# The first cross attention of a Perceiver kernel, its steps of one key group put together into rounds of two

## What is computed

```python
def _L0_xattn_ref(x, y, wq, bq, wk, bk, wv, bv, wo, bo):
    N_HEADS, D_EMBED, D_HEAD = 16, 256, 16
    B, SQ, _ = x.shape
    SKV = y.shape[1]
    q = (x @ wq + bq).reshape(B, SQ, N_HEADS, D_HEAD)
    k = (y @ wk + bk).reshape(B, SKV, N_HEADS, D_HEAD)
    v = (y @ wv + bv).reshape(B, SKV, N_HEADS, D_HEAD)
    scores = jnp.einsum('bqhd,bkhd->bhqk', q, k) / jnp.sqrt(jnp.asarray(D_HEAD, x.dtype))
    attn = jax.nn.softmax(scores, axis=-1)
    out = jnp.einsum('bhqk,bkhd->bqhd', attn, v).reshape(B, SQ, D_EMBED)
    return out @ wo + bo

x = x + _L0_xattn_ref(_layernorm(x, axis=-1), ctx_768, ...)
```

## Time and profile before

| | |
|---|---|
| runs | 2088.68, 2086.16, 2082.78 us |
| profiled execution, own time | 2083.18 us |
| its span, first to last instruction | 2081.4 us |
| TensorE busy | 1893.3 us, 91% |
| VectorE, ScalarE, GpSimd busy | 1301.7, 924.8, 678.0 us |
| first look_at to last look_at of this stage | 31.36 to 692.65 us |
| project of the last tile | 717.86 us |
| granted TensorE clock, mean | 0.955 |

### The profile page before, as it was taken

One profiled execution on the slowest core, in us unless ns is written; L12 is line 12 of the kernel. 1 busy time (PEld: TensorE's weight loads), 2 busy tenths in 40 slices (PEclk: granted clock), 3 DMA queues, 4 the chain that ended last, 5 costly groups with the idle time before them and its releaser, 6 DMA issues.

```text
span 2081.4 us, 44041 instructions
## 1 busy us (share of the span) xinstructions
PE 1893.3 (91%) x17906; PEld 1569.1 (75%) x17906; DVE 1301.7 (63%) x2827; ACT 924.8 (44%) x1952; POOL 678.0 (33%) x762
## 2 busy tenths in 40 slices
PE   6999999999999688795999999999999989779994
PEld 4777777777777477685999999999999846546662
DVE  5777877777777765543767667676676536532222
ACT  4666666666665423343444444444444324212221
POOL 4444444444443322104323333233333014130002
PEclk9999999999999888887999999999999989799997
DMA  6211111111200200104223222232222070310002
GB/s 199 65 34 34 34 57 42 34 34 34 65 2 3 93 1 1 49 1 113 56 56 90 77 56 56 56 97 70 56 56 56 1 280 2 121 59 31 31 29 71
DMA packets 55655, 119.81 MB, mean 58 GB/s; under 512 B 4432, under 2 KB 41888, under 8 KB 53920
## 3 DMA queue, kind: packets, MB, share of 16 engines
q1 hardware_dynamic: 53920, 112.80, 18.1%
q0 software_dynamic: 1536, 4.20, 0.6%
HBM read 107.80 MB, written 9.18 MB: 56 GB/s over the span
## 4 chain that ended last, share of the span: by engine, by line
PE 72%; DVE 15%; ACT 6%; issue 4%; DMA 1%; POOL 1%; SPq 0%; POOLq 0%; DVEq 0%; ACTq 0%
PE ps L104 8%; PE ps L163 7%; PE ps L433 6%; PE ps L2106 6%; PE ps L472 5%; DVE arena L531 4%; PE ps L1314 4%; PE ps L456 4%; PE ps L2130 3%; PE ps L1315 3%; PE ps L450 2%; DVE arena L1407 2%; PE ps L1272 2%; PE ps L1300 2%; PE ps L1299 2%
## 5 line engine op out<-in xcount | busy, mean ns | idle before, releaser
L531 DVE TENSOR_REDUCE arena<-ps 128x1 f32<-128x400 f32 (+1 forms) x512 | 258.4, 567 | 136.8 <-PE ps L433 136.8
L651 ACT ACTIVATE arena<-ps 128x384 f32<-128x384 f32 (+1 forms) x512 | 223.4, 522 | 102.5 <-PE ps L456 102.5
L1314 PE MATMUL ps<-arenaR 128*128 128x386 f32 x768 | 246.5, 356 | 1.1 <-DVE arenaR L1401 1.1
L1500 ACT CAST arenaR<-ps 128x512 fp32r<-128x512 f32 (+1 forms) x256 | 116.7, 508 | 225.0 <-PE ps L163 225.0
L1315 PE MATMUL ps<-arenaR 128*128 128x256 f32 x768 | 215.6, 281 | 0.0
L557 DVE TENSOR_TENSOR arena<-arena 128x512 f32<-128x512 f32 x192 | 176.7, 920 | 5.3 <-ACT arena L651 1.7
L1543 POOL TENSOR_TENSOR arenaR<-h,arenaR 128x400 fp32r<-128x400 f32 (+1 forms) x60 | 57.9, 964 | 370.5 <-ACT arenaR L1485 370.5
L709 POOL TENSOR_TENSOR arena<-arena 128x512 f32<-128x512 f32 (+1 forms) x96 | 134.0, 1396 | 101.9 <-ACT arena L651 99.5
L1401 DVE TENSOR_TENSOR arenaR<-ps,arenaR 128x512 fp32r<-128x512 f32 (+1 forms) x256 | 138.8, 584 | 25.3 <-ACT arenaR L1500 24.9
L682 POOL TENSOR_TENSOR arenaR<-arena,arenaR 128x400 fp32r<-128x400 f32 x64 | 67.1, 1049 | 256.1 <-ACT arenaR L617 255.8
L1383 DVE TENSOR_TENSOR arenaR<-wsb,arenaR 64x400 fp32r<-64x400 f32 x64 | 66.0, 1035 | 133.3 <-ACT arenaR L1486 133.3
(11 more groups left out here) (316 smaller groups left out, 4591.6 us busy)
## 6 DMA issues: line engine op xcount, KB each, us to landing
wsb<-in_ctx SPq DMA_DIRECT2D x16, 1152.0 KB
arena<-in_ctxT SPq DMA_DIRECT2D x16, 800.5 KB, 5.0
arena<-in_ctxT SPq DMA_DIRECT2D x32, 400.2 KB, 7.2
wsb<-in_ctxT SPq DMA_DIRECT2D x32, 400.2 KB, 7.5
gu<-in_m_gu SPq DMA_DIRECT2D x8, 1536.0 KB, 19.6
h<-in_ctxT SPq DMA_DIRECT2D x15, 800.5 KB, 5.0
dn<-in_m_dn SPq DMA_DIRECT2D x8, 768.0 KB, 9.2
xs_rows<-zeros SPq DMA_DIRECT2D x1, 2944.0 KB, 15.7
```

The lines of the kernel that those rows point to most:

```text
L531: e.tensor_reduce(mx4[n % 2][:, u, i:i + 1], ps[:, at("look", n, i, u), 0:400 + (i == 3)], AX.X, ALU.max).then_inc(c.maxed.at((n, i, u)), 1)
L651: e.activation(v[:, u, 0:128 * GN[s]], ps[:, at("st", n, s, u), 0:128 * GN[s]], ACT.Exp).then_inc(c.exp_a.at((x0, n, s, u)), 1)
L1314: e.matmul(o, PTh[:, t, :], v[:, t, 0:386], start=(t == 0), stop=False)
```

## The change

The loops of all engines run over rounds r of two key groups in place of steps of one. In round r TensorE does: scores of the first group, look_at of one chunk, values of both groups of round r - 1 (and total behind those of a second half), scores of the second group, look_at of another chunk; then the turn, two chunks of keys, two pieces of vals, and now and then queries or project.

With it: the sums of values leave bank 7. Each round's sums take a bank of the ring, which is now round all 8, and ScalarE copies it out (`take_sum`) to new tiles `va` (first half of the unit) and `vb` (second half, with the denominators). `normalise` reads those, adds the halves with one more instruction and divides. The gathering of sums of P is shared otherwise: VectorE has 4 adds a unit where it had 7, GpSimd 6 where it had 4. The projection is added to x on VectorE one round after TensorE made it, and TensorE's `project` stands at the end of a round r divisible by 8, in which `normalise` of the unit it needs also stands.

```diff
     V = [ar(128, KT, 256) for _ in range(2)]
     P = [ar(128, 4, 512) for _ in range(3)]
     acc_d, acc_p = ar(128, 4, 128), ar(128, 4, 128)
+    va, vb = ar(128, 128), ar(128, 256)
...
     N = 2 * NB
     G0, GN = (0, 4, 7, 10), (4, 3, 3, 3)
-    FIRST, LAST = -6, 16 * (NT - 1) + 18
+    FIRST, LAST = -3, 2 * N
...
+    def groups(r):
+        return [(r // 2, 2 * (r % 2) + i) for i in range(2)] if 0 <= r < 2 * N else []
+    def looks(r):
+        return [((r + 3) // 2, 2 * ((r + 3) % 2) + i) for i in range(2)] if 0 <= (r + 3) // 2 < N else []
+    def keys_of(r):
+        return [((r + 4) // 2, 2 * (r % 2) + i) for i in range(2)] if 1 <= (r + 4) // 2 < N else []
+    def vals_of(r):
+        b, p = (r + 4) // 4, 2 * ((r + 4) % 4)
+        return [(b, i) for i in (p, p + 1) if i < 7] if 0 <= b < NB else []
+    def turns(r):
+        return (r + 1) // 2 if r % 2 and 0 <= (r + 1) // 2 < N else None
+    def asks(r):
+        return (r + 5) // 8 if (r + 5) % 8 == 0 and 1 <= (r + 5) // 8 < NT else None
+    def projects(r):
+        return r // 8 - 1 if r % 8 == 0 and 1 <= r // 8 <= NT else None
     bank = {}
     def at(*use):
         if use not in bank:
-            bank[use] = len(bank) % 7
+            bank[use] = len(bank) % 8
         return bank[use]
     for i in range(4):
         at("k", 0, i)
-    at("v", 0, 0)
+    for i in range(2):
+        at("v", 0, i)
...
+    for r in range(FIRST, LAST + 1):
+        for i in range(2):
+            for n, s in groups(r)[i:i + 1]:
+                for u in range(4):
+                    at("st", n, s, u)
+            for n, k in looks(r)[i:i + 1]:
+                for u in range(4):
+                    at("look", n, k, u)
+            if i == 0 and r >= 1:
+                at("sum", r - 1)
+        if turns(r) is not None:
+            at("m", turns(r))
+        for use in keys_of(r):
+            at("k", *use)
+        for use in vals_of(r):
+            at("v", *use)
+        if asks(r) is not None:
+            at("q", asks(r))
+        if projects(r) is not None:
+            at("o", projects(r))
...
-    def splits(s):
-        b, i = (s + 14) // 8, (s + 14) % 8
-        return (b, i // 2) if i % 2 == 0 and 1 <= b < NB else None
+    def splits(r):
+        b, i = (r + 7) // 4, (r + 7) % 4
+        return (b, i) if 1 <= b < NB else None
...
-        def values(n, s):
+        def values(r):
+            n, half = r // 2, r % 2
             b, f = n // 2, 128 * (n % 2)
-            w.wait_ge(*c.exp_a((x0, n, s, 3)))
+            w.wait_ge(*c.exp_a((x0, n, 2 * half + 1, 3)))
             w.wait_ge(*v_out((b, 6)))
-            if s == 0 and n:
-                w.wait_ge(*c.o_out((x0, n - 1)))
-            for t in range(GN[s]):
-                k = G0[s] + t
-                r = 128 if k < 12 else KL
-                for u in range(4):
-                    a = e.matmul(ps[32 * u:32 * u + 32, 7, 0:128], V[b % 2][0:r, k, f + 32 * u:f + 32 * u + 32],
-                                 P[(4 * n + s) % 3][0:r, u, 128 * t:128 * t + 128], start=(k == 0), stop=(k == 12))
-            a.then_inc(c.summed.at((x0, n, s)), 1)
-        def total(n):
-            w.wait_ge(*added_d((n, 3)))
-            w.wait_ge(*added_p((n, 3)))
-            w.wait_ge(*padded("rows"))
-            for a, v in enumerate((acc_d, acc_p)):
-                for u in range(4):
-                    o = e.matmul(ps[32 * u:32 * u + 32, 7, 128:256], ones, v[:, u, :], start=(a == 0), stop=(a == 1))
-            o.then_inc(totals.at(n), 1)
+            bk = take("sum", r)
+            for s in (2 * half, 2 * half + 1):
+                for t in range(GN[s]):
+                    k = G0[s] + t
+                    rows = 128 if k < 12 else KL
+                    for u in range(4):
+                        a = e.matmul(ps[32 * u:32 * u + 32, bk, 0:128], V[b % 2][0:rows, k, f + 32 * u:f + 32 * u + 32],
+                                     P[(4 * n + s) % 3][0:rows, u, 128 * t:128 * t + 128], start=(k == 7 * half), stop=(k == 6 + 6 * half))
+                a.then_inc(c.summed.at((x0, n, s)), 1)
+            if half:
+                w.wait_ge(*added_d((n, 3)))
+                w.wait_ge(*added_p((n, 3)))
+                w.wait_ge(*padded("rows"))
+                for a, v in enumerate((acc_d, acc_p)):
+                    for u in range(4):
+                        o = e.matmul(ps[32 * u:32 * u + 32, bk, 128:256], ones, v[:, u, :], start=(a == 0), stop=(a == 1))
+                o.then_inc(totals.at(n), 1)
+            emptied[bk] = c.o_out((x0, r))
...
+        for r in range(FIRST, LAST + 1):
+            for i in range(2):
+                for use in groups(r)[i:i + 1]:
+                    scores(*use)
+                for use in looks(r)[i:i + 1]:
+                    look_at(*use)
+                if i == 0 and r >= 1:
+                    values(r - 1)
+            if turns(r) is not None:
+                turn_m(turns(r))
+            for use in keys_of(r):
+                keys(*use)
+            for use in vals_of(r):
+                vals(*use)
+            if asks(r) is not None:
+                queries(asks(r))
+            if projects(r) is not None:
+                project(projects(r))
...
-                for t in range(2):
+                for t in range(2 if s == 2 else 1):
                     w.wait_ge(*added_d.now())
                     e.tensor_tensor(acc_d, acc_d, v[:, :, 128 * t:128 * t + 128], ALU.add).then_inc(added_d.at((n, s)), 1)
         def normalise(n):
             b, g = n // 2, n % 2
             q = slice(64 * (b % 2), 64 * (b % 2) + 64)
-            w.wait_ge(*totals(n))
-            e.reciprocal(rS, ps[:, 7, 128:256]).then_inc(c.dv.at(), 1)
+            w.wait_ge(*c.o_out((x0, 2 * n + 1)))
+            e.reciprocal(rS, vb[:, 128:256]).then_inc(c.dv.at(), 1)
+            e.tensor_tensor(oS, va, vb[:, 0:128], ALU.add).then_inc(c.dv.at(), 1)
             w.wait_ge(*c.dv.now())
-            e.tensor_tensor(oS, ps[:, 7, 0:128], rS, ALU.mult).then_inc(c.o_out.at((x0, n)), 1)
-            w.wait_ge(*c.o_out((x0, n)))
+            e.tensor_tensor(oS, oS, rS, ALU.mult).then_inc(c.dv.at(), 1)
+            w.wait_ge(*c.dv.now())
             w.wait_ge(*c.in_const("small"))
             e.tensor_scalar(o1, oS[:, 0:64], c.par[:, 0:1], c.bvc[:, g:g + 1], ALU.mult, ALU.add).then_inc(c.dv.at(), 1)
             w.wait_ge(*c.dv.now())
...
+        for r in range(FIRST, LAST + 1):
+            if asks(r - 1) is not None:
+                queries(asks(r - 1))
+            if projects(r - 1) is not None:
+                project(projects(r - 1))
+            for use in looks(r)[:1]:
+                maxima(*use)
+            for use in groups(r)[:1]:
+                add(*use)
+            for use in looks(r)[1:]:
+                maxima(*use)
+                if use[1] == 3:
+                    maximum(use[0])
+            if r >= 2 and r % 2 == 0:
+                normalise(r // 2 - 1)
+            for use in groups(r)[1:]:
+                add(*use)
+        project(projects(LAST))
...
+        def take_sum(r):
+            n = r // 2
+            w.wait_ge(*(totals(n) if r % 2 else c.summed((x0, n, 1))))
+            if n:
+                w.wait_ge(*c.o_norm((x0, n - 1)))
+            v = vb if r % 2 else va
+            e.copy(v, ps[:, at("sum", r), 0:256 if r % 2 else 128]).then_inc(c.o_out.at((x0, r)), 1)
...
+        for r in range(FIRST, LAST + 1):
+            for use in groups(r)[:1]:
+                exps(*use)
+            if r >= 1:
+                take_sum(r - 1)
+            for use in groups(r)[1:]:
+                exps(*use)
+            if turns(r) is not None:
+                turn_m(turns(r))
+            for use in keys_of(r):
+                keys(*use)
+            if splits(r) is not None:
+                split(*splits(r))
+            for use in vals_of(r):
+                vals(*use)
...
-                r = 128 if s < 3 else KL
-                w.wait_ge(*added_p.now())
-                e.tensor_tensor(acc_p[0:r], acc_p[0:r], v[0:r, :, 256:384], ALU.add).then_inc(added_p.at((n, s)), 1)
+                for t in range(2 if s == 2 else 1, GN[s]):
+                    k = 128 if G0[s] + t < 12 else KL
+                    w.wait_ge(*added_p.now())
+                    e.tensor_tensor(acc_p[0:k], acc_p[0:k], v[0:k, :, 128 * t:128 * t + 128], ALU.add).then_inc(added_p.at((n, s)), 1)
...
+        for r in range(FIRST, LAST + 1):
+            for use in groups(r)[:1]:
+                add(*use)
+            if r % 2 == 0 and 1 <= (r + 4) // 2 < N:
+                blockdiag((r + 4) // 2)
+            for use in groups(r)[1:]:
+                add(*use)
+            if splits(r) is not None:
+                split(*splits(r))
...
```

More of the change, by code:

```diff
@@ L305, in latents @@
     at("q", 0)
-    for s in range(FIRST, LAST + 1):
-        if has_look(s):
-            for u in range(4):
-                at("look", *look(s), u)
-        if has_key(s):
-            at("k", *key(s))
```

(76 more changed lines are left out.)

20 lines of the change are left out of this document (removed).

## The result

The changed kernel took 2078.22 us (median of 8 runs, 2073.04 to 2081.89) against 2086.78 beside it: ratio 0.9963, interval 0.9949 to 0.9977. Faster, but by 8.6 us where 41 were forecast.

A forecast was written before the change was run, and what follows sets the result against it. TensorE's own work was taken as the bound, some 40.8 of 42.6 us a batch. 42.6 - 2.8 - 1.8 + 2.1 = 40.1 over 15 batches, with the ends 40 us less in all: 2045 us, range 2033 to 2057.

The forecast's parts named there:

- (b): End of a round with project: TensorE waits for VectorE's normalise, 1.0 us once in two batches, 0.5 a batch.
- the walk: Even round followed in us from its first scores: TensorE reaches project at 10.1, VectorE's normalise ends at 11.1.
- (c): Odd round's first maxima queue behind normalise and an add on VectorE, whose adds stretch beside GpSimd: 1.0 us a batch.
- Changes of cut: TensorE switching between whole array, rows and columns: four a round, not eight; 0.70 us less, 2.8 a batch.
- The waits of before: TensorE's waits for VectorE in the kernel before (maxima, values and total), all taken off: 1.8 us a batch.
- (a): Values wait for the sums' bank, still read by exponentials of the round's first scores: 0 to 0.15 us, 0.4 a batch.
- (d): Short round: the next look waits for the bank that ScalarE's copy of vals, behind split, frees late: 0.2 us a batch.
- The ends: Start and end of the stage: fewer changes at the start save 1 us, fewer VectorE adds at the end 1.5.
- rival B: VectorE and GpSimd block each other in the even round: waits 4.0, 42.0 us a batch, 2075 us; chance 0.14.
- A: TensorE alone sets the rate: waits 0.5, 38.5 us a batch, 2021 us; chance 0.27.
- C: Late maxima hold banks: TensorE waits 2.7 us twice a batch, 5.5 with (a); 43.5 a batch, 2097 us; chance 0.06.
- D: Looks behind scores still show weight loads (sign: a look at 0.89): 41.6 us a batch, 2068 us; chance 0.08.

The follow-up runs named there:

- e1: The changed kernel with TensorE's project one round later: 2052.78 us, ratio 0.9857 to the kernel before.
- e10: The changed kernel with normalise ahead of the second look's maxima on VectorE in even rounds, project left in place: 2057.85 us, ratio 0.9869.
- e2: The changed kernel with the adds of P shared as before, 7 a unit on VectorE and 4 on GpSimd: 2075.38 us, ratio 0.9954.
- e3: The changed kernel with GpSimd's adds after the first of a unit cut to one column in 128: 2063.69 us, ratio 0.9914.
- the extra matmul: Two runs on e1 with one more 64-column matmul a round between the chunks of keys: on one strip 2074.02 us, on the whole array 2061.47 us.
- e11: The changed kernel with both moves, normalise ahead of the second maxima and project one round later: 2052.36 us, ratio 0.9839.
- e4: The changed kernel with look_at ahead of scores in both halves of a round, the ring's order swapped likewise: 2117.30 us, ratio 1.0148.
- e12: e10 with the bank of a round's sums dealt ahead of the scores' banks: 2237.77 us, ratio 1.073.
- e9: e1 with normalise moved to the end of odd rounds, va and vb doubled, project two rounds later: 2087.68 us, ratio 1.0011.

## Why the prediction was wrong

The forecast was 2.5 us a batch over 15 batches. Measured over the same 15, from first scores to first scores: 42.5 - 41.8 = 0.7. The failed step is (b), the price of project's wait. I gave it 1.0 a pair; the changed kernel without it (e1) is 4.0 a pair and 25.4 us faster, and e10, which removes the wait otherwise, 20. Over the 15 batches that is 25.6 us where I had 7.5: 18 of the 27 us by which they fell short. Two things were missing in (b):

- Its first part was 2.2 and not 1.0. Counted from a round's first scores, the walk had the second maxima end at 7.9, the maximum at 8.5, normalise at 11.1, and TensorE ready at 10.1. In the round before the wait that ends at 310 they are 8.1, 9.8, 12.6 and 10.4. So nearly all of it is the maximum, 1.7 for 0.6, by one subtraction. I had seen that two-input instructions are stretched and put 0.3 on each in (c), a mean that takes in times with GpSimd idle. But the place is fixed: GpSimd's two adds start with the same exponentials each round, so L552 meets the second one 30 times of 30 (1265 ns; 168 ns before, 0.17 in e2 and e3). I charged the stretch to (c), the next maxima, and forgot that project stands in the same queue.
- I took a wait as its length. A TensorE that stood 2.2 us was then given half the clock for 3.4 us, after five of seven waits, and that costs 1.5 us each time: the same kind of batch takes 45.0 with it and 43.5 without. No row of before showed that in the stage; behind the last look, at 704 to 707 us, it has such a stretch.

With these two the 25.6 us by which e1's 15 batches are shorter come out: seven waits of 2.23 are 15.6, five halved stretches of 1.5 are 7.5, a look's strip that stands 0.7 to 0.8 us once, at 316, is 0.8 (what it waits for the profile doesn't show), and 0.24 a pair is left, 1.7.

The other terms fell short by 9 us together. Without (b) the forecast is 39.6 a batch, and e1, where (b) is absent, takes 40.1 on the mean. That this is the very 40.1 of the forecast is luck.

- Changes of cut, 0.70 a round: by the shortest starts of each group a round saves 0.58, 2.3 a batch and not 2.8. The price itself was too high (two that the extra matmul adds cost 0.31 and not the 0.40 that the same prices give), and the look's part is off: a look behind scores takes 0.865 to the next start (249.66 to 250.53) where 0.89 was before and 0.7 foretold. Its first pass got 0.10 cheaper (0.34 for 0.44), its second 0.08 dearer, and I have not found why. Scores came out as said: 24 of them 0.67, where 0.77 were the earlier trace rows.
- The waits of before, of which I took off 1.8 a batch: by starts TensorE's groups stood 1.3 a batch over their shortest. The two rows for L450 in the earlier trace rows, matmuls and weight loads, tell in part of the same time, and I added them.
- (a), the sums' bank: 43 us of waiting weight loads in 60 rounds, but only 0.3 to 0.4 us a batch beyond the shortest such step. As forecast (0.4).
- (c), the odd round: the last strips of its second look start late, the step takes 1.27 to 1.31 and not 0.87, so 0.8 a batch (forecast 1.0). It is not shown that this is VectorE's lateness alone. In e10, where VectorE is free earlier, the look takes 0.96, but the turn behind it (L163) takes 0.29 to 0.38 to the first keys and not 0.08. TensorE's starts in e1, then in e10:

```profile
244.94 1.38 PE L441 MATMUL ps<-arena 32*128 32x400 f32 x8
246.25 0.33 PE L163 MATMUL ps<-ident,arenaR 128*128 128x128 f32 x1
246.33 0.43 PE L392 MATMUL ps<-arenaR 128*128 128x400 f32 x1
```

```profile
267.00 0.84 PE L439 MATMUL ps<-arena 32*128 32x400 f32 x8
267.96 0.30 PE L163 MATMUL ps<-ident,arenaR 128*128 128x128 f32 x1
268.34 0.42 PE L390 MATMUL ps<-arenaR 128*128 128x400 f32 x1
```

From the look to the second matmul of keys it is 1.62 to 1.66 us in e1 and 1.53 to 1.60 in e10, so an earlier VectorE gives back only 0.1 to 0.2 of the 0.8. The rest goes with the turn's new place, a term that the sum doesn't have: between keys and vals, where it stood before, it added 0.11 us, and right behind a look it adds 0.4 in e10 (1.2 without a turn). Whether the keys wait for a bank there, the profile doesn't tell.
- (d), 0.2 a batch, I did not measure apart. The ends: the first scores come 1.8 us later where I had 1 saved, and from the last unit's first scores to the last project nothing is saved where I had 1.5. The last scores come 8.6 us earlier, the last project 7.8. Behind the stage, from 900 to 1200, 5 of 9 us went back; the clock stood at half for 61 of the 360 us from 850 to 1210, 55 before; e1 kept its gain there better (35.6, then 31 us). That part I leave open.

By number rival B came nearest (42.0 a batch, 2075), and its block is there in every round. But e1 leaves the block as it is and gets 25 us back, so it costs through project and the clock, which B did not price. A's 2021 no kernel here reached; e1 and e11 end at 2052 to 2053, nearer the forecast itself. C did not happen. D did not either, although its sign, a look of 0.89, nearly came: the look's weight loads run beside the scores, and the time is at the look's end. In C's sum two waits of 2.7 with (a) are 5.8 and not 5.5; it changes nothing here.

## What to carry over

When a consumer is moved behind its producer's queue into the same round, walk that queue by the instructions that collide each time, not by a mean stretch, and ask what it costs if the array stands for 2 us: more than 2 us. And before a ring of banks is dealt anew, name for each wait whose content was there last; twice here (e4, e12) another order of the ring made a fresh content the one waited for. One round of distance for an occasional step (project) was worth three times the change itself (25.4 us and 8.6).

## What was unexpected of the hardware

- The granted clock fell to half for 3.4 us after idle stretches of only 1.9 to 2.3 us in an otherwise full stage: five of seven in the changed kernel, seven of seven in e9. After idle stretches of 1.7 us it was one of seven in e3 and none of seven in e2. In e1, without such idle stretches, there was none between 24 and 665 us.
- A VectorE subtraction of 128 x 4 with two inputs in SBUF took 1265 ns on the mean beside GpSimd's adds and 0.17 us without them; it ends when the add of 1.3 us ends. The Trainium skill, SBUF — State Buffer, section SBUF: two separate sides, says that the port is held for the whole instruction, and the trace agrees.
- Two changes of the array's cut in whole-array work cost 0.31 us: 0.09 up to the strip's matmul, 0.20 from it to the next start, 0.02 behind that.
- A look that follows scores in the same cut enters 0.10 us cheaper and ends 0.08 us dearer, so standing side by side saved it almost nothing (0.865 for 0.884).
